# A vision layer with the first pairs' grey on VectorE, the key projection as three fp32r products, and a new order of work

## What is computed

```
gray = 0.2989 r + 0.587 g + 0.114 b
h = sum over both Scharr kernels of |conv3x3(gray)| / 2
n = layernorm(h)                              # rows are 256 tokens of 256 channels
xk, xv, xr = n * tm + shift(n) * (1 - tm)     # shift: the token before
k, v, r = xk Wk', xv Wv', xr Wr'
wkv = RWKV recurrence over tokens (running maximum, two scans)
h = h + (sigmoid(r) * wkv) Wo'
n2 = layernorm(h)
e = argmax(n2 Wg')                            # one of 8 experts a token
h = h + gelu((layernorm(n2) scale_e + bias_e) W1_e + b1_e) W2_e + b2_e
```

## Time and profile before

| | |
|---|---|
| median of 3 runs | 1195.4 us (1194.34 to 1196.62) |
| profiled execution, its own time | 1192.2 us |
| its span | 1190.7 us |
| TensorE, VectorE, ScalarE, POOL busy | 93%, 84%, 72%, 15% of the span |
| mean granted TensorE clock | 0.981 |
| first convolution | 48.9 us |

### The profile page before, as it was taken

How to read it: one execution, slowest core, us unless ns; L and a number is a source line. 1 busy time by engine, 2 the same in 40 slices (tenths; PEclk the granted TensorE clock), 3 DMA queues, 4 the chain that set the end, 5 groups by cost and what they waited for, 6 DMA issues and landing times.

```text
span 1190.7 us, 16854 instructions
## 1 busy us (share of the span) xinstructions
PE 1109.3 (93%) x5571; PEld 696.7 (59%) x5571; DVE 1003.7 (84%) x1828; ACT 858.2 (72%) x1380; POOL 177.3 (15%) x242
## 2 busy tenths in 40 slices
...
GB/s 187 207 169 121 133 127 128 149 154 140 136 151 150 139 134 134 158 143 135 147 146 146 132 129 159 153 132 136 158 145 123 137 149 153 141 102 47 18 18 36
DMA packets 164837, 157.79 MB, mean 133 GB/s; under 512 B 12528, under 2 KB 164678, under 8 KB 164678
## 3 DMA queue, kind: packets, MB, share of 16 engines
...
## 4 chain that ended last, share of the span: by engine, by line
PE 90%; DMA 3%; DVE 3%; ACT 2%; SPq 1%; issue 0%; POOL 0%; POOLq 0%; DVEq 0%
PE bank L1008 28%; PE bank L1144 18%; PE bank L1074 15%; PE bank L1002 10%; PE bank L1050 9%; PE bank L1096 4%; DMA rows_in<-gray_dram 2%; PE bank L1122 2%; PE bank L1145 1%; DMA gray_dram<-planes 1%; PE bank L1087 1%; PE bank L1131 1%; PE bank L1063 1%; SPq L329 1%; DMA scharr_dj<-in_L_tok_scharr_dram 0%
## 5 line engine op out<-in xcount | busy, mean ns | idle before, releaser
L1144 PE MATMUL bank<-w_sb,hidden 128*128 128x256 f32 x1024 | 238.8, 380 | 0.8 <-ACT hidden L860 0.8
L1144 PEld LDWEIGHTS bank<-w_sb,hidden 128*128 128x128 f32 x1024 | 184.6, 190 | 29.2 <-ACT hidden L860 1.5
L1002 PE MATMUL bank<-rows_in,conv_w 102*32 102x512 f32 x1024 | 129.9, 628 | 31.5 <-DMA rows_in<-gray_dram 31.5
L1008 PE MATMUL bank<-mixed_k,w_k_t 128*128 128x512 f32 x256 | 127.5, 622 | 4.1 <-DVE mixed_k L557 4.1
L1008 PE MATMUL bank<-mixed_r,w_r_t 128*128 128x512 f32 x256 | 118.6, 607 | 4.8 <-DVE mixed_r L557 4.8
L1074 PE MATMUL bank<-normed_hi,w_hi 128*128 128x512 f32 x256 | 122.2, 477 | 0.0
L1008 PE MATMUL bank<-mixed_v,w_v_t 128*128 128x512 f32 x256 | 120.1, 592 | 0.0
L568 DVE TENSOR_TENSOR_SCAN max_state<-neg_exp_w,bank 128x256 f32<-128x256 f32 x128 | 80.7, 672 | 45.3 <-PE bank L1008 45.3
L1050 PE MATMUL bank<-w_o_t,rwkv 128*128 128x256 f32 x512 | 117.5, 382 | 0.0
L403 POOL TENSOR_TENSOR pool_turn<-pool_turn 128x1 f32<-128x1 f32 x32 | 7.9, 246 | 663.1 <-ACT planes L784 663.1
L1050 PEld LDWEIGHTS bank<-w_o_t,rwkv 128*128 128x128 f32 x512 | 94.9, 190 | 12.0 <-issue 0.5
...
## 6 DMA issues: line engine op xcount, KB each, us to landing
rows_in<-gray_dram SPq DMA_DIRECT2D x192, 256.0 KB
planes<-in_x_dram SPq DMA_DIRECT2D x128, 256.0 KB, 5.0
gray_dram<-planes POOLq DMA_DIRECT2D x128, 256.0 KB, 6.1
gray_dram<-in_x_dram SPq DMA_DIRECT2D x64, 256.0 KB, 6.5
out_dram<-resid SPq DMA_DIRECT2D x64, 256.0 KB, 2.2
rows_in<-gray_dram SPq DMA_DIRECT2D x128, 24.0 KB
...
hidden<-in_L_ffn_W_dram SPq DMA_DIRECT2D x2, 256.0 KB, 10.3
```

Source lines behind the costliest of these rows:

```text
L1002: ins = pe.matmul(bank[BANK_EDGE[n]][ROW_TILE * q:ROW_TILE * (q + 1), :], conv_w[0:TAPS, c, :], rows, start=True, stop=True)
L1008: ins = pe.matmul(ps[:, :], w_t[i][:, kt, ct * P:(ct + 1) * P], mixed[i][:, 2 * kt:2 * kt + 2, :].rearrange("p i t -> p (i t)"), start=(kt ...
L1144: pe.matmul(ps, hidden[:, m, i, rows], w2_sb[:, m, :], start=(m == 0), stop=False)
```

## The change

**Grey of the first two pairs** (`FIRST = 2`): all three planes are loaded into SBUF, half 0 by SP and half 1 by ScalarE's queue. VectorE makes the grey rows in two passes a half (`first_gray_of`) in memory of the second `rows_in`; they are stored to `gray_dram` and read back, each by both queues. The zero borders are two small stores instead of a megabyte. The other 30 pairs keep their way, but red and green planes are loaded with a wait between them. `rows_in` has two buffers, so rows of one pair can land while the other's are convolved.

**Key projection**: `w_k` and the mixed input are split into a part rounded to fp32r and the rest. Four fp32 matmuls a pair become twelve fp32r products. For this ScalarE copies the mix (`high_part`) and VectorE subtracts the copy (`low_part`) for every pair.

**Order**: all engines' `step` is reordered, PSUM banks are given out anew, and four buffers are shared (`mixed_k` with `gap`, `step_diff` with `normed`, `num_state` with `den_state`, `w_k_t` with `den`). The log of the denominator, the logits and their copy move from the end of a step to the start of the next. Setup of the weights, which was ahead of the steps or of step 2 and 3, stands in step 2 and before steps 3 and 4 on VectorE; eight small parameter loads and `Wr` are issued by ScalarE.

The diff, cut to its core:

```diff
-        rows_in = sb("rows_in", [P, TILES, 2, D])
+        rows_in = [sb(f"rows_in{i}", [P, TILES, 2, D]) for i in range(2)]
...
-        step_diff = sb("step_diff", [P, NB, T])
-        mixed = [sb(f"mixed_{n}", [P, NB, T]) for n in "kvr"]
+        step_diff = normed
         gap = sb("gap", [P, NB, T])
+        mixed = [gap] + [sb(f"mixed_{n}", [P, NB, T]) for n in "vr"]
...
-        num_state = sb("num_state", [P, NB, T + 1])
+        num_state = den_state
...
+        part_hi = {i: sb(f"part_{'kvro'[i]}_hi", [P, NB, T], F32R) for i in SPLIT}
+        part_lo = {i: sb(f"part_{'kvro'[i]}_lo", [P, NB, T], F32R) for i in SPLIT}
...
+        w_hi = {i: sb(f"w_{'kvro'[i]}_hi", [P, CH, D], F32R) for i in SPLIT}
+        w_lo = {i: sb(f"w_{'kvro'[i]}_lo", [P, CH, D], F32R) for i in SPLIT}
...
+        def store_first(eng, i, half):
+
+            dst = gray_dram[i, :, 1 + half * P:1 + (half + 1) * P, :].rearrange("i p w -> p i w")
+            eng.wait_ge(s_first_zeros, 1)
+            eng.wait_ge(s_first_gray, HALF * i + half + 1)
+            eng.dma_start(dst, first_gray[i][:, 2 * half:2 * half + 2, :]).then_inc(first_stored[i], 16)
+
...
+            load_first(sp, 0, 0)
+            load_first(sp, 1, 0)
+            store_first(sp, 0, 0)
+            sp.wait_ge(s_borders, 16)
+            sp.wait_ge(first_stored[0], 16 * HALF)
+            load_rows(sp, 0, 0)
+            store_first(sp, 1, 0)
...
+            sp.wait_ge(first_stored[1], 16 * HALF)
+            load_rows(sp, 1, 0)
...
+                if at.has_later(LOAD):
+                    b = at.buf(LOAD)
+                    wait(sp, s_green, at.count(LOAD, 16 * HALF, 16 * HALF, back=2 + FIRST))
+                    if at.is_step(2) or at.is_step(3):
+                        sp.wait_ge(s_first_gray, HALF * (at.u - 1))
+                    load_plane(0, at.j, at.u, b)
+                    wait(sp, s_edge_ps, at.count(LOAD, 4, 4, back=3))
+                    load_plane(1, at.j, at.u, b)
+                    wait(sp, rows_loaded[b], at.dma_count(LOAD, X_DMAS, back=2))
+                    load_blue(at.j, at.u, b)
+                if at.has_later(GRAY):
                     b = at.buf(GRAY)
+                    wait(sp, s_green, at.count(GRAY, 16 * HALF, 16 * HALF, back=FIRST))
+                    if not at.has(LOAD):
+                        wait(sp, s_edge_ps, at.count(GRAY, 4, 4, back=2))
                     for i in range(2):
+                        load_rows(sp, b, i)
...
+            def first_gray_of(i):
+
+                for half in range(HALF):
+                    rows = slice(2 * half, 2 * half + 2)
+                    total = first_gray[i][:, rows, 1:D + 1]
+                    dve.wait_ge(first_in[i][half], 48)
+                    dve.scalar_tensor_tensor(out=total, in0=planes[i][:, rows, 0, :],
+                                             scalar=GRAY_WEIGHTS[0] / GRAY_WEIGHTS[2], in1=first_blue[i][:, rows, :],
+                                             op0=ALU.mult, op1=ALU.add).then_inc(s_first_mix, 1)
+                    dve.wait_ge(s_first_mix, HALF * i + half + 1)
+                    dve.scalar_tensor_tensor(out=total, in0=planes[i][:, rows, 1, :],
+                                             scalar=GRAY_WEIGHTS[1] / GRAY_WEIGHTS[2], in1=total,
+                                             op0=ALU.mult, op1=ALU.add).then_inc(s_first_gray, 1)
+
+            first_gray_of(0)
...
+                if i in SPLIT:
+                    done(dve.tensor_copy(w_hi[i][:, :, :], w_t[i][:, :, :]))
+                    done(dve.tensor_tensor(w_lo[i][:, :, :], w_t[i][:, :, :], w_hi[i][:, :, :].bitcast(F32), ALU.subtract))
...
+            def low_part(i, stage, low_done, at):
+                if not at.has(stage):
+                    return
+                if i == 0:
+                    wait(dve, s_high_k, at.count(stage, 1, 1))
+                dve.tensor_tensor(part_lo[i][:, :, :], mixed[i][:, :, :], part_hi[i][:, :, :].bitcast(F32),
+                                  ALU.subtract).then_inc(low_done, 1)
...
+            load_first(act, 0, 1)
...
+            load_first(act, 1, 1)
+            act.wait_ge(s_first_zeros, 1)
+            act.dma_start(bass.AP(gray_dram.tensor, 0, [[IMAGE, 4], [(T + 1) * PITCH, 2], [1, PITCH]]),
+                          zero_rows.unsqueeze(1).to_broadcast([4, 2, PITCH])).then_inc(s_borders, 16)
+            store_first(act, 0, 1)
+            act.wait_ge(s_borders, 16)
+            act.wait_ge(first_stored[0], 16 * HALF)
+            load_rows(act, 0, 1)
+            store_first(act, 1, 1)
...
+            def high_part(i, stage, high_done, at):
+                if not at.has(stage):
+                    return
+                if i == 0:
+                    wait(act, s_mix_k, at.count(stage, 1, 1))
+                act.activation(part_hi[i][:, :, :], mixed[i][:, :, :], ACT.Copy).then_inc(high_done, 1)
...
             def project(i, ct, ps, ps_done):
+                products = [(w_t[i], mixed[i])]
+                if i in SPLIT:
+                    products = [(w_hi[i], part_hi[i]), (w_lo[i], part_hi[i]), (w_hi[i], part_lo[i])]
                 for kt in range(CH):
-                    ins = pe.matmul(ps[:, :], w_t[i][:, kt, ct * P:(ct + 1) * P],
-                                    mixed[i][:, 2 * kt:2 * kt + 2, :].rearrange("p i t -> p (i t)"),
-                                    start=(kt == 0), stop=(kt == CH - 1))
+                    for n, (weights, part) in enumerate(products):
+                        ins = pe.matmul(ps[:, :], weights[:, kt, ct * P:(ct + 1) * P],
+                                        part[:, 2 * kt:2 * kt + 2, :].rearrange("p i t -> p (i t)"),
+                                        start=(kt == 0 and n == 0), stop=(kt == CH - 1 and n == len(products) - 1))
                 ins.then_inc(ps_done, 1)
...
             def step(at):
+                route_logits(at)
                 convolve(0, at)
                 convolve(1, at)
                 transpose_logits(at)
+                convolve(2, at)
                 project_k(0, at)
-                convolve(2, at)
+                project_k(1, at)
                 convolve(3, at)
-                project_k(1, at)
-                project_v(0, at)
-                transpose_route(at)
+                first_layer(0, at)
+                experts_ready(at)
                 output_projection(0, at)
                 output_projection(1, at)
-                first_layer(0, at)
+                project_v(0, at)
+                first_layer(1, at)
+                first_layer(2, at)
+                transpose_route(at)
+                project_v(1, at)
                 mask_out(at)
-                first_layer(1, at)
-                project_v(1, at)
-                first_layer(2, at)
+                project_r(0, at)
                 first_layer(3, at)
-                project_r(0, at)
+                transpose_normed2(0, at)
                 project_r(1, at)
-                transpose_normed2(0, at)
+                setup_experts(at)
                 transpose_normed2(1, at)
                 second_layer(0, at)
+                setup_projections(at)
                 transpose_normed(0, at)
                 transpose_normed(1, at)
                 second_layer(1, at)
-                route_logits(at)
```

455 lines of the change are left out of this document (245 added, 210 removed).

## The result

The changed kernel took 1179.44 us (median of 4 runs, 1175.35 to 1180.26) against 1194.87 (4 runs, 1193.26 to 1196.62) for the one before: ratio 0.9864, 95% interval 0.9836 to 0.9891. It is faster by 15 us, where 50 were forecast, and outside the range. In a later comparison of the same two it was 1179.17 against 1192.36 (0.9881, 0.9858 to 0.9905).

What follows compares the result with a forecast made beforehand. TensorE was taken to bound the steps, between a start of chained latencies and a tail. Gains of 22, 23.5 and 4 made 49.5 from 1192.2 us: 1142.7, forecast as 1145 since the median is 3.2 higher; range 1131 to 1168.

Steps and rivals of the forecast that it cites:

- the grey chain: Rival in the steps: the loop from convolutions through scaling to the next rows sets the step; 1218 us, chance 0.04.
- k0: First half of the key projection in a step; its start was forecast at 46 us first, then 79 in step 4.
- The steps, 23.5 forecast: Repeating steps on a full TensorE: 27 steps, each 0.87 us shorter through the split key projection, 32.95 us a step.
- since the other matmuls are the same and only their order changes: TensorE in a step: reordering costs nothing, so 0.87 us of the key projection's gain of 0.88 was taken.
- The second rival: Key projection: three products no faster, since each change between fp32 and fp32r costs; up to 0.8 us, 1171, chance 0.08.
- The start, 22 forecast: Start: first convolution 24 us earlier, 27 us gained at step 4's keys, 5 given back by VectorE; 22 us gained.
- my lower bound: Least gain expected in the start: 14 us, with late first rows and VectorE's full bound.
- The bound of 32: Start: latest first convolution, at 32 us, if the second pair's loads hold up store and rows; 24 to 25 expected.
- the fourth rival: Start: first pairs' store and rows crawl behind weights and pair 1; 14 us gained instead of 22, 1153, chance 0.07.
- Scaling now ends at about 48: Step 4 in the start: ScalarE's scaling of pair 2 ends at 48 instead of 68.3, rows there at 74 to 78.
- The tail, 4 gained forecast: From step 33's keys to the end: 1.7 us from keys and 2.3 from the route's waits, together 4; bounds 1 and 6.
- k's 0.87 twice: Tail: the key projection's gain of 0.87 us a step counted for two more steps, 1.7 us.

Runs made afterwards that it cites:

- a removal: The changed kernel with the fourth convolution moved ahead of the key projection, so all convolutions stand together: 1169.64 us, ratio 0.9815 against the kernel before.
- an addition: The changed kernel with the last convolution cut in two, half of it behind the first part of the first layer: 1213.07 us, ratio 1.0185 against the kernel before.
- the three together: The changed kernel with pair 1's loads behind pair 0's stores, later weights before step 3, and step 3's scaling ahead of the high part: 1174.07 us, ratio 0.983.

## Why the prediction was wrong

**Right.** TensorE bounds the steps (840.00 of 840.00 us), products start 0.23 us apart, VectorE has idle time left (794.14 of 840), and the grey chain doesn't set the step. In the start, planes and grey came as worked out (forecast 12, in the trace 11.3), and from the first convolution to the first k0 passed 20.7 us (21.5 forecast).

**The steps, 23.5 forecast, 9.1 measured.** The failed step is "since the other matmuls are the same and only their order changes". The order alone costs 0.37 us a step, as the run without the split shows, and the split is worth 0.70 instead of 0.87: I priced twelve products at the spacing they have among themselves, while as a group between convolutions they pay on entering and leaving. The second rival had the right suspicion and the wrong kind. Going from fp32 to fp32r costs nothing where v and the first layer meet (641.78 to 646.26 is 4.48 us: 1.72, which half a projection takes elsewhere, and 12 x 0.23). What costs is going into and out of the convolution's narrow tile (102x32), 0.1 us each way, shown by a removal, by an addition, and by the fp32 keys of the run without the split. The Trainium skill (TensorEngine Tiling (Array Packing), Key Properties) says that changing the tiling mode drains TensorE; the 0.1 us each way agree with it, and the page, which gives no figure, would have told me the sign of the term that I set to zero. The other 0.14 of the order's cost is not taken apart. The timeline has v's second half at 1.87 behind the route's bf16 transposes and r's first at 1.82 behind the mask, instead of 1.72; but the mask is both bf16 and in a tile of its own (32x128), and behind the single bf16 matmul of the second layer nothing is lost, so which change costs there stays open.

**The start, 22 forecast, 8.6 measured, under my lower bound.** Two terms were mis-sized. Store and rows were taken with landing times from the middle of the program: 12 to 25, measured 11.3 to 33.4. The row loads ran at a DMA share of 0.99; the stores did not, for the share was 0.35, 0.80, 0.65 and 0.11 in the four stretches of 3 us from 9 to 21, and why they still took over 8 us is open (with pair 1's loads behind them it was 2.8 less). The bound of 32 nearly held that, and the fourth rival had named it. The other was wrong in kind: "Scaling now ends at about 48". I followed the pair's data and not SP's queue, where pair 2's planes stand behind W1 and b2, 12.35 us of issue; scaling ended at 59.3 and step 4 began at 89 instead of 74 to 78. The runs show that SP's order and ScalarE's order hold it together: the weights' move alone gains nothing, that of pair 1's loads 2 to 3 us at this place, and the three together 5 to 6. What holds the rest is most likely the DMA traffic, which wasn't tested. The Trainium skill (DMA: Bandwidth & Descriptors, Issuing engines are not separate DMA queues) had said that a second issuing queue moves nothing faster; the DMA shares of 0.99 from 20 to 34 us and 1.21 from 36 to 48 agree, and more of the forecast should have been read from it: in these stretches the second queue has nothing left to win.

**The tail, 4 gained forecast, 5.4 lost.** Two steps failed. The larger is the order, from which I kept 2.3: without the split it loses 3.6. The route's waits of 2.38 and 1.37 are gone, but TensorE now waits 2.11 and 1.11 for normed2's low part, 0.69 twice for the copied route and 2.4 in all for gelus (0.78 before), and the low clock behind the first of these adds some 1.5 us in step 35. The other is "k's 0.87 twice": I costed the low part's wait for steps that have convolutions and carried the gain into steps that have none. The cover is gone there, 1.97 us of wait and 1.2 of slow products in step 34, so that the split loses 1.8 on top.

**What wasn't named.** That the split would need the reorder (0.09 without it) stands nowhere in the prediction; it took both as independent and the reorder as free.
